# A delta-rule layer on one core: the recurrence without a loop, its inverses in two transfers per half step, values and mixed terms for two half steps per transfer

## What is computed

```
q, k, v = silu(short_conv(x @ W.T, taps))          # three projections, 4 taps
delta   = delta rule over chunks of 32 positions:  # per batch and head
    A = tril(-(k*beta) @ k.T, -1);  T = inv(I - A);  u = T @ (v*beta);  w = T @ (k*beta)
    for each chunk:  u' = u - w @ S;  o = q @ S + tril(q @ k.T) @ u';  S = S + k.T @ u'
o = p0*fir3(v) + p1*fir15(v) + p2*fir63(v) + p3*delta + p4*v      # p: softmax gates
x1 = layernorm(x + rmsnorm(o) @ Wo.T)
out = layernorm(x1 + ffn(x1))                      # gated, two hidden layers of 1024
```

## Time and profile before

| | us |
|---|---|
| time, median of 3 runs | 2368.65 (2364.51 to 2372.69) |
| time of the profiled execution | 2375.07 |
| its span, from first to last instruction | 2373.2 |
| stages 1 and 2, until the barrier | 0 to 581 |
| `delta`: first state addition to last | 604.46 to 1009.65 |
| first product of `ffn` by its weights | 1055.24 |

### The profile page before, as it was taken

How to read it: one execution, slowest core, us unless ns; L and a number is a source line. 1 busy time by engine, 2 the same in 40 slices (tenths; PEclk the granted TensorE clock), 3 DMA queues, 4 the chain that set the end, 5 groups by cost and what they waited for, 6 DMA issues and landing times.

```text
span 2373.2 us, 43639 instructions
## 1 busy us (share of the span) xinstructions
PE 2094.9 (88%) x16936; PEld 1776.2 (75%) x16936; DVE 1159.3 (49%) x1825; ACT 864.9 (36%) x1406; POOL 529.7 (22%) x563
## 2 busy tenths in 40 slices
PE   7888873775888878759999999999999999999998
PEld 5776763675777767648888888888888888888886
DVE  5777768953467657642432343233234324432332
ACT  4545542010333323223443444344334434443442
POOL 1113787864445444410000000000000000000000
PEclk9999996797899988869999999999999999999999
DMA  3775667876778777750000000000000000000000
GB/s 123 199 199 171 200 191 182 284 255 207 201 216 221 210 214 205 209 216 34 19 0 18 18 15 3 18 18 0 18 18 18 0 18 18 10 8 18 18 1 18
DMA packets 244242, 237.59 MB, mean 100 GB/s; under 512 B 145938, under 2 KB 203794, under 8 KB 238354
## 3 DMA queue, kind: packets, MB, share of 16 engines
q1 hardware_dynamic: 227218, 193.74, 28.0%
q10 hardware_dynamic: 16896, 41.95, 5.7%
HBM read 139.96 MB, written 95.68 MB: 99 GB/s over the span
## 4 chain that ended last, share of the span: by engine, by line
PE 53%; issue 1%; DVE 1%; ACT 1%; DMA 0%; POOL 0%; DVEq 0%; SPq 0%; ACTq 0%; POOLq 0%
PE B L1636 48%; PE O L1664 5%; PE T L1592 1%; DVE yb L1763 0%; ACT gate L1702 0%; DMA x<-x_s 0%; DVE stats L1794 0%; ACT L1702 0%; DVE z L1789 0%; DVE xl L1743 0%; DVE z L1785 0%; DVE z L1808 0%; ACT xh L1690 0%; POOL rstd L1844 0%; DVEq L1758 0%
## 5 line engine op out<-in xcount | busy, mean ns | idle before, releaser
L1636 PE MATMUL B<-act1l,wr 128*128 128x512 f32 x1024 | 398.4, 389 | 0.0
L1636 PE MATMUL B<-act0h,wr 128*128 128x512 f32 x1024 | 398.3, 389 | 0.0
L1636 PE MATMUL B<-act0l,wr 128*128 128x512 f32 x1024 | 398.3, 389 | 0.0
L1636 PE MATMUL B<-act1h,wr 128*128 128x512 f32 x1024 | 398.3, 389 | 0.0
L1716 ACT ACTIVATE yb<-B,scol 128x512 f32<-128x512 f32 x256 | 176.2, 688 | 581.0 <-PE B L1636 581.0
L1751 DVE TENSOR_TENSOR act0l<-yb,act0h 128x512 fp32r<-128x512 f32 x256 | 176.1, 688 | 377.8 <-ACT act0h L1719 375.7
L1841 POOL TENSOR_TENSOR rstd<-mv,ln_eps 128x4 f32<-128x4 f32 x16 | 3.2, 199 | 1308.2 <-DVE mv L1802 1308.2
L449 DVE SCALAR_TENSOR_TENSOR acc<-proj,taps,acc 128x512 f32<-128x512 f32 x288 | 214.3, 750 | 86.4 <-ACT acc L395 77.9
L1751 DVE TENSOR_TENSOR act1l<-yb,act1h 128x512 fp32r<-128x512 f32 x128 | 88.6, 692 | 295.5 <-ACT act1h L1719 295.5
L1636 PEld LDWEIGHTS B<-act0h,wr 128*128 128x128 f32 x1024 | 192.2, 188 | 39.9
L1636 PEld LDWEIGHTS B<-act1h,wr 128*128 128x128 f32 x1024 | 192.2, 188 | 39.9
(11 more groups left out here) (171 smaller groups left out, 3234.5 us busy)
## 6 DMA issues: line engine op xcount, KB each, us to landing
qk_s<-yT SPq DMA_DIRECT2D x16, 1024.0 KB, 6.3
kk_s<-kfull SPq DMA_DIRECT2D x16, 1024.0 KB, 6.3
qk<-qk_s SPq DMA_DIRECT2D x32, 512.0 KB, 5.3
wraw<-in_ffn_w ACTq DMA_DIRECT2D x32, 352.0 KB, 6.1
wr_s<-wround ACTq DMA_DIRECT2D x32, 352.0 KB, 4.0
toe<-in_toe_short ACTq DMA_DIRECT2D x32, 320.0 KB, 7.4
xt<-in_xt SPq DMA_DIRECT2D x16, 524.0 KB, 4.3
k_s<-ktok SPq DMA_DIRECT2D x16, 512.0 KB, 7.1
```

Of the source, the lines that this page charges most:

```text
L1636: last = nc.tensor.matmul(B[slot % 4][:, :], w, part, start=(k == 0 and i == 0), stop=(k == kts - 1 and i == len(parts) - 1))
```

## The change

- All half steps of `delta` are written out on all engines; there is no loop, no register and no counting semaphore `passed` left there.
- The inverses lie in HBM in another way. Of the four blocks q of a matrix, `g_s` holds blocks 0 and 2 as they are and 1 and 3 turned; `f_s` holds 0 and 2 turned, and zeros in 1 and 3. A half step's blocks then come in two transfers over all 128 partitions (`f_s` to the left half of `tt`, `g_s` to the right) in place of six over 32 partitions each. `first_inv` is gone: `first_round` reads its block from the right half of `tt`, where `second_out` later puts the joined block.
- `vtok` and `mix` are one tensor each with the ring as a dimension. One half step's transfer brings the 64 rows of both pairs of batches, that is for two half steps at once (`slots_in`); where the ring ends, once in four half steps, it is two. It stands at the end of SyncE's step, behind a wait for `mixed` of this half step.
- Stage 1 stores zeros in blocks 1 and 3 of `f_s` (8 transfers of 256 KB). Stage 2 stores three sets of 2 blocks for each half of the inverses in place of two of 4.

```diff
@@ project, SyncE
+                for first in range(0, GRP, WIN):
+                    for q in range(1, NQ, 2):
+                        sp.dma_start(io["f_s"][first:first + WIN, q, :, :].rearrange("n i j -> n (i j)"),
+                                     zero[:, :, :].rearrange("p h d -> p (h d)")).then_inc(zero_stored, 16)
@@ weights_fir, SyncE
-                        blocks_out("d_s", tri[:, D_OUT[n]:SLOTS:NSUB, :, :], D_OUT[n], inv_stored)
+                        blocks_out("g_s", 0, tri[:, D_OUT[n]:SLOTS:2 * NSUB, :, :], D_OUT[n], inv_stored)
...
-                        blocks_out("t_s", turned_inv[:, :, :, :], T_OUT[n], turned_stored)
+                        blocks_out("g_s", 1, turned_inv[:, 1:NQ:2, :, :], T_OUT[n], turned_stored)
+                        blocks_out("f_s", 0, turned_inv[:, 0:NQ:2, :, :], T_OUT[n], turned_stored)
@@ delta, SyncE, group_in
-                        sp.dma_start(tt[r][j, :, 0:CH], io["t_s"][mats, 2 * c].rearrange("s i j -> i s j")
-                                     ).then_inc(prep_in[p], 16)
-                        sp.dma_start(tt[r][i, :, CH:HC], io["t_s"][mats, 2 * c + 1].rearrange("s i j -> i s j")
-                                     ).then_inc(prep_in[p], 16)
-                        sp.dma_start(first_inv[p][j, :, :], io["d_s"][mats, 2 * c].rearrange("s i j -> i s j")
-                                     ).then_inc(prep_in[p], 16)
+                    for half, name in enumerate(("f_s", "g_s")):
+                        sp.dma_start(tt[r][:, :, half * CH:half * CH + CH], io[name][mats].rearrange("s q i j -> (q i) s j")).then_inc(prep_in[p], 16)
+                def slots_in(part, t):
+                    rows, u = slice(part * HC, part * HC + HC), 2 * t + part
+                    for first, end in ((0, GB), (GB, BATCH)) if u % RING == RING - 1 else ((0, BATCH),):
+                        r = (u + first // GB) % RING
+                        places = slice(r, r + (end - first) // GB)
+                        sp.dma_start(vtok[rows, :, places, :, :].rearrange("p h r b d -> p h (r b d)"),
+                                     io["v_s"][:, rows, t + 1, first:end, :].rearrange("h p b d -> p h (b d)")).then_inc(slots[part][t % 2], 16)
+                        sp.dma_start(mix[rows, places, :, :, :].rearrange("p r b h d -> p (r b h) d"),
+                                     io["mix_s"][part, t, first:end, :, :, :].rearrange("b h m d -> m (b h) d")).then_inc(slots[part][t % 2], 16)
@@ delta, SyncE, step
                     sp.wait_ge(s_ready, u + 1)
-                    sp.sem_inc(passed, 1)
-                    sp.wait_ge(mixed, u)
-                    sp.sem_inc(passed, 1)
-                    sp.wait_ge(prep_done, u + 2)
-                    sp.sem_inc(passed, 1)
...
-                        slot_in(0, (r + 3) % RING, (r + 3) % 2, n + 2 if r % 2 else n + 1, (r + 3) % 2)
-                        slot_in(1, (r + 3) % RING, (r + 3) % 2, n + 1, r % 2)
...
+                    sp.wait_ge(mixed, u + 1)
+                    t = n + 2 if u % 2 else n + 1
+                    if t < STEPS:
+                        slots_in(1 - u % 2, t)
@@ delta, TensorE, first_round
-                            last = nc.tensor.matmul(NA[rows, 0, c, :], lt[r % 2][rows, c, :], first_inv[r % 2][rows, c, :],
+                            last = nc.tensor.matmul(NA[rows, 0, c, :], lt[r % 2][rows, c, :], tt[r][rows, c, CH:HC],
@@ delta, every engine (here SyncE; TensorE, ScalarE, VectorE and GpSimd likewise)
-                for u in range(3):
+                for u in range(GROUPS):
                     step(u, u % RING, u // 2)
-                u = steps(sp, step, 3, GROUPS - 3)
-                while u < GROUPS:
-                    step(u, u % RING, u // 2)
-                    u += 1
```

More of the change, by code:

```diff
@@ L912, in delta @@
             st.sem(f"p3_{n}") for n in ("power_set", "par_in", "wo_done", "ready", "tables_done"))
-        prep_in, vt_in, x_in, mix_in = (st.pair(f"p3_{n}_in") for n in ("prep", "vt", "x", "mix"))
+        prep_in, x_in = (st.pair(f"p3_{n}_in") for n in ("prep", "x"))
+        slots = [st.pair(f"p3_slots{n}_in") for n in range(2)]
         fs_ready, q_ready, n_ready, a_ready, y_ready, s_ready, o_ready, t_ready, w_ready = (
@@ L926, in delta @@
             st.sem(f"p3_{n}") for n in ("total_summed", "total_ready", "flag_done", "flag_stored"))
-        passed = st.sem("p3_passed")
-        NPREP = 10
+        NPREP = 6
         LAST = GROUPS
         def rows_of(u):
[L934 to L942, removed]
+            return slice(0, HC) if u == 0 else slice(HC, P) if u == LAST else slice(0, P)
         with nc.Block() as block:
@@ L1044, in chunks @@
                     new, old = (r, 0, slice(0, HC)), ((r - 1) % RING, 1, slice(HC, P))
-                    return [new] if isinstance(u, int) and u == 0 else [old] if isinstance(u, int) and u == LAST else [new, old]
+                    return [new] if u == 0 else [old] if u == LAST else [new, old]
                 def tokens(k, half):
@@ L1093, in solve @@
                     pe.wait_ge(x_done, u + 1)
[L1094 removed]
+                    if u != LAST:
                         pe.wait_ge(a_out, u + 1)
[L1096 removed]
                     for k in range(GK):
@@ L1153, in step @@
                 def step(u, r, n):
-                    early, late = isinstance(u, int) and u < 2, isinstance(u, int)
-                    prep = not late or u + 1 < GROUPS
+                    prep = u + 1 < GROUPS
                     from_state(u, r)
@@ L1161, in step @@
                     queries_state(u, r)
-                    if not late or u >= 1:
+                    if u >= 1:
                         turn(u - 1, (r - 1) % RING)
-                    if not late or u < LAST:
+                    if u < LAST:
                         new_state(u, r, n)
@@ L1179, in _ @@
                     step(u, u % RING, u // 2)
-                u = steps(pe, step, 3, GROUPS)
-                while u <= LAST:
-                    step(u, u % RING, u // 2)
-                    u += 1
                 turn(LAST, LAST % RING)
@@ L1235, in step @@
                 def step(u, r, n):
-                    prep = not isinstance(u, int) or u + 1 < GROUPS
+                    prep = u + 1 < GROUPS
                     if prep:
@@ L1269, in _ @@
                 second_out(0, 0)
-                for u in range(3):
+                for u in range(LAST + 1):
                     step(u, u % RING, u // 2)
-                u = steps(act, step, 3, GROUPS)
-                while u <= LAST:
-                    step(u, u % RING, u // 2)
-                    u += 1
                 turned_out(LAST, LAST % RING)
@@ L1341, in outputs @@
                     dve.wait_ge(o_done, u + 1)
-                    nc.vector.tensor_tensor(of, of, mix[r][rows, :, :, :].rearrange("p b h d -> p (b h) d"), ALU.add).then_inc(mixed, 1)
+                    nc.vector.tensor_tensor(of, of, mix[rows, r, :, :, :].rearrange("p b h d -> p (b h) d"), ALU.add).then_inc(mixed, 1)
                 def compare_weights(c, r):
@@ L1403, in _ @@
                 nc.vector.tensor_scalar(wo[:, :, :], wo_raw[:, :, :], norm_w[:, 0:1], None, ALU.mult).then_inc(wo_done, 1)
-                for u in range(3):
-                    step(u, u % RING, u // 2)
-                u = steps(dve, step, 3, GROUPS)
-                while u <= LAST + 2:
+                for u in range(LAST + 3):
                     step(u, u % RING, u // 2)
@@ L1457, in step @@
                 def step(u, r, n):
[L1458 to L1459 removed]
+                    if u + 1 <= LAST:
                         pool.wait_ge(x_done, u)
                         prep(u + 1, (r + 1) % RING, n + 1 if r % 2 else n)
[L1462 to L1465 removed]
+                    if u >= 3:
+                        tail(u - 3, (2 * u - 2) if u <= LAST else LAST + u - 1)
+                    if u <= LAST:
+                        norm(u, 2 * u - 1 if u >= 3 else u + 1)
                 prep(0, 0, 0)
[L1468 removed]
+                for u in range(LAST + 3):
                     step(u, u % RING, u // 2)
[L1470 to L1473 removed]
 def ffn(nc, sems, io, keep):
```

131 lines of the change are left out of this document (46 added, 85 removed).

## The result

The changed kernel takes 2351.82 us (median of 9 runs, 2330.38 to 2361.49) against 2368.43 of the kernel before beside it, a ratio of 0.9903 with a 95% interval of 0.9879 to 0.9928. It is faster, as forecast, but by 17 us where 73 were forecast, and 2352 lies outside the range of 2266 to 2336. The profiled execution took 2355.54 us, 19.5 less than that of before.

What follows compares the result with a forecast made beforehand. SyncE's queue was taken to bound `delta`. Savings of 67.3 us (half steps), 3 (start) and 2.5 (stage 2) sum to 72.8: 2375.07 to 2302.3 profiled, 2296 after 6.4 us to the median; range 2266 to 2336.

Steps and rivals of the forecast that it cites:

- The diff leaves that stage alone: `ffn`, from 1055.24 us on: TensorE busy 1302.86 of 1317.96 us, code untouched, so no time to win there.
- The new half step: `delta`: 10.4 us by the DMA engines plus 0.5 for stops, 10.9 in place of 13.07, saving 67.3 us.
- Either way SyncE is below 10.18 us and stops being the bound: SyncE's queue in `delta`: 10 or 12 transfers in place of 16, 6.3 us a half step, 8.7 at the upper bound.
- My own sign for this: SyncE's issues in `delta`: the new transfers' price is wrong if `tt` holds SyncE for over 1.2 us each.
- The DMA engines as a floor: `delta`: 10.2 us a half step plus 0.5 for short rows, 10.7 by share, 10.4 at full share 1.03.
- Rival B: `delta`: DMA engines don't fill, share 0.90, half step 11.9 us, 2327 us (2312 to 2345); chance 0.20.
- The new wait: SyncE in `delta`: `vt` and `mix` behind `mixed` have a whole half step, 10 us, as cover; costed at nothing.
- The loop: TensorE in `delta`: 5.5 us for each time around go, within the 13.07, so not counted again.
- Start and stage 2: `delta` starts 3 us earlier with fewer issues; stage 2's second store takes 2.5 us less.
- C: `delta`: TensorE's chain bounds, undisturbed 10.18 us nearly throughout, 10.3 us a half step, 2277 us; chance 0.16.
- D: `delta`: slower, DMA share stays at 0.78, half step 13.7 us, 2383 us; chance 0.05.
- E: `delta`: no change, instruction fetches on TensorE replace the loop's stops, half step 13.1 us, about 2364 us; chance 0.04.

Runs made afterwards that it cites:

- 256 increments: Changed kernel with 256 short semaphore increments run on TensorE ahead of `ffn`: `ffn` 1336.0 us, ratio 1.0018 to the kernel before.
- 167: Changed kernel with that many increments ahead of `ffn`'s loop: run, `ffn` 1319.2 us, ratio 0.9918; in the branch not taken, 1318.8 us, 0.9856.
- 174: Kernel before with that many increments in `ffn`'s branch that isn't taken: `ffn` 1343.6 us, whole 2394.2 us, ratio 1.0087.
- `slots_first`: Changed kernel, `ffn`'s loop at its good place, SyncE issuing values and mixed terms ahead of its other loads: half step 11.84 us, ratio 0.9844.
- `tt_on_act`: Changed kernel, `ffn`'s loop at its good place, ScalarE issuing the two `tt` loads: half step 10.39 us, whole 2285.85 us, ratio 0.9657.
- `tt_act_order`: Changed kernel with ScalarE issuing `tt` and SyncE issuing values and mixed terms at the head of its step: half step 11.68 us, ratio 0.9798.

## Why the prediction was off

**"The diff leaves that stage alone", "none in `ffn`".** This step failed: 18.6 us were lost there. The code was left alone but its place in the instruction stream was not, and `ffn`'s loop sits on the bound of the stage, TensorE, which had no stop of this kind before and now has one of some 2 us in each turn. It is shown by shifts alone, in both directions. The same stops that the prediction priced at the end of `delta`'s loop should have been asked for in every other loop. The Trainium skill ("Runtime: NRT & Kernel Launch", Instruction fetch mechanics) says that TensorE has room for 2048 instructions filled in blocks of 256 and that a branch out of the window stalls. By it a loop of some 1630 spans seven or eight such blocks by its place, an estimate. That 256 increments changed nothing and 167 and 174 did agrees with blocks of 256, and 1.02 MB in 62 fetches with the page's 16 KiB for one; the page doesn't say why one place is fetched again in each turn (nine times) and another never, and no run here shows the room itself.

**The new half step, 10.9 us.** This term was mis-sized: 11.85 in the profiled execution (11.16 to 12.26 in five), 37.7 us saved where 67.3 were forecast. The step in it that failed is "Either way SyncE is below 10.18 us and stops being the bound". I took the holds of its issues as each transfer's own price, 0.6 us for `tt` and 0.5 for `xres`. As prices in a queue with less in it these were right: 0.60 and 0.45 were measured with `tt` on ScalarE, and 0.62 for `tt` on SyncE without `qk`. But SyncE goes on issuing without a break with 10.5 transfers, and the holds grew to 2.35 for the second `tt`, above my upper bound of 1.8, and 1.63 for `xres`; all together they are 10.6 us of a half step where I had 5.7. My own sign for this, `tt` holding SyncE for over 1.2 us each, came true: the two take 1.5 us each on average. The earlier trace rows had shown it: in the half step behind the loop that took 14.23 us the sixteen holds are 13.3 us, grown as the gaps fell, and I read it as "fewer transfers may, if it isn't the DMA engines that hold it". It was not the number of issues. Nor were the engines together full: with `tt` on another queue they moved more. ("Once in 380 us" for SyncE's waits leaves out two of 0.5 and 0.2 us; nothing hangs on it.)

**The DMA engines as a floor, 10.4 us.** The 0.50 us for the short rows were about right (10.3 - 10.0 = 0.3). The values' transfers, given nothing, added 1.1 us of packet time. But packet time is no fixed work: with the same transfers, share by half step is 11.5 us in `slots_first`, 10.9 in `tt_on_act` and 10.4 in `tt_act_order`, so a floor worked out from it moves with the order and the queues. 1.03 as full fits `tt_on_act`, which reaches 1.04; with these loads all in SyncE's queue the whole change stayed at 0.92 to 0.95 in four executions of five and reached 1.00 in one.

**Rival B.** By time the result is B's (2312 to 2345 once `ffn`'s 18.6 us are off, and 11.9 us a half step), and one of its two signs is there, SyncE issuing without a break. The other isn't: the share is 0.95, not below 0.92. That its 11.9 us came out is in part luck, as 10.7 / 0.90 stands against 11.3 / 0.95 measured. I gave it 0.20 and argued against it that the new transfers hold four times the rows for less issue time; they took more issue time, 2.35 us for the second of the two.

**The new wait, priced at nothing.** It did appear, 55.1 us in 11 waits and the 53.4 us beside them, with SyncE late, which the prediction had named as the condition. Taking it away brought nothing that can be measured, so it isn't the cause of the miss.

**The loop.** "Written-out code alone doesn't free the queue" holds in so far as data are late with it; yet it alone brought 13.07 (12.70 to 13.22 in three executions) to 12.29 us in profiled executions and 0.4% in time, where I counted nothing for it.

**Start and stage 2, 5.5 us.** In the changed kernel the first product is at 589.64 in place of 592.22, and the first state addition no earlier. Over twelve traces with the new inverses' transfers it lies at 601.4 on average (599.7 to 604.8), over seven without at 606.0 (604.5 to 607.3): 4.5 us, right in size.

**C, D and E.** C's chain of 10.18 us is real, 10.05 with no data late; with all data loaded only `tt_on_act`, with a second queue, came near it (10.39). D's ceiling of 0.78 and E's stops in each half step did not show.

What stays open: which property of the one queue limits it. Number of rows and bytes both seem to count (`tt` moved 10.39, `qk` moved 11.30, `qk` left out 10.42), and no run separates how many requests may stand in it from how fast it works through them. Nor is it settled why one execution of the same kernel took 11.16 us a half step and another 12.26, which places of `ffn`'s loop are bad, and why less of `ffn`'s 17 us than the traces show came back in the whole time.

## What to carry to other kernels

When code ahead of a loop changes in length, read the instruction queue's fetches in that loop before and after, above all in a stage where TensorE has no gaps; increments in a branch that isn't taken, which never run, put it back here. An issue that holds its engine for long can be a sign of a full queue rather than of a dear transfer: see whether cheap transfers behind it are held too, and try the one with the most rows on another engine's queue before making transfers fewer. A floor from the DMA share holds for the engines together; ask what share a single queue has ever reached. And when a term of a sum is a hold, ask what it becomes when others go: here it filled the time that they left.

## What the runs showed of the hardware

A stage whose TensorE loop has some 1630 instructions took 1318 to 1320 us or 1334 to 1344 us by the loop's place, with 7 to 9 or some 60 fetches; a turn took 163.4 us with no fetch, and 165.6 to 166.8 with nine in the changed kernel.

Moving two transfers of 128 KB each of a half step from SyncE's to ScalarE's queue raised what all DMA engines moved from 234 to 267 GB/s (SyncE's queue 172 in both, ScalarE's from 60 to 92) and the kernel's speed by 2%. The Trainium skill ("DMA: Bandwidth & Descriptors", Rules for kernel authors) has it that spreading transfers over issuing engines doesn't help bandwidth and only saves issue time, because all share the same 16 engines. Issue time was saved here, and more than the moved transfers' own: SyncE's holds fell from 10.6 to 5.0 us of a half step. Two loads also landed sooner after their issue (from 620 to 930 us, medians): `qk` 4.4 in place of 7.4 us, `kt` 4.3 in place of 7.0. Others didn't: `xres` 4.7 in place of 4.6, the store `x_s` 4.4 in place of 3.5, ScalarE's `wr_s` 6.4 in place of 4.9. So where the rule says that bandwidth doesn't rise, the measurement decides, for a queue that is always issuing and has many short rows; how much of the rise is saved issue time isn't separated.
